# Behind the attention: order and queues of the loads, the projection out in the same block, and the borders beside the projection up

## What is computed

```
x = x + dwconv(x, pos_w, pos_b)
xn = layer_norm(x, ln1_g, ln1_b)
...                                   # q, k, v of 12 heads of 8 channels; lepe = dwconv(v, lepe_w, lepe_b)
attn = jax.nn.softmax(qk, axis=-1)
o = jnp.einsum('bnlm,bnmd->bnld', attn, vr)
o = o.transpose(0, 2, 1, 3).reshape(B, H, W, C) + lepe
x = x + (o @ out_w + out_b)
xn = layer_norm(x, ln2_g, ln2_b)
h = jax.nn.gelu(xn @ fc1_w + fc1_b, approximate=False)
h = h + dwconv(h, dw_w, dw_b)
x = x + (h @ fc2_w + fc2_b)
```

## Time and profile before

| | |
|---|---|
| median of the runs, us | 3207.21 |
| profiled execution, us | 3203.94 |
| its span, us | 3202.2 |
| mean granted clock of TensorE, share of 2.4 GHz | 0.717 |
| busy: PE, DVE, ACT, POOL | 93%, 80%, 55%, 33% |
| block behind the attention and projection out | 878.1 to 939.3 us |
| layer norm | 939.6 to 969.5 us |
| block of the borders and the gates' loads | 970.6 to 979.2 us |
| projection up starts | 979.7 us |

### The profile page before, as it was taken

The page is one execution under the profiler, slowest core; times in us unless marked ns, Lnnn a source line. Parts: engine busy times, 40 slices in busy tenths (PEclk is TensorE's granted clock), DMA queues, the critical chain, the costliest instruction groups (busy, mean ns, idle before and its releaser), DMA issues. The chain is left out here.

```text
span 3202.2 us, 127142 instructions
## 1 busy us (share of the span) xinstructions
PE 2988.6 (93%) x50420; PEld 2307.2 (72%) x50420; DVE 2551.8 (80%) x12130; ACT 1746.9 (55%) x5568; POOL 1050.1 (33%) x2510
## 2 busy tenths in 40 slices
PE   6799999999857989999999999999999999779987
PEld 3365656666523359999999999999999999455654
DVE  6799999999865678888888888888888888598872
ACT  2599999999803144444444444444444444344443
POOL 2478777778600012222222222222222222100000
PEclk8899999999968975555555555555555555689999
DMA  2323323333230000000000000000000000000000
GB/s 64 97 93 117 116 92 118 99 110 117 62 86 20 12 1 4 4 4 4 4 4 4 4 4 4 4 4 4 4 4 4 4 4 4 2 1 1 1 6 15
DMA packets 48217, 104.74 MB, mean 33 GB/s; under 512 B 11305, under 2 KB 18793, under 8 KB 47692
## 3 DMA queue, kind: packets, MB, share of 16 engines
q1 hardware_dynamic: 32796, 45.53, 5.0%
q0 software_dynamic: 13824, 50.34, 4.4%
q10 hardware_dynamic: 1072, 1.60, 0.2%
HBM read 84.06 MB, written 13.37 MB: 30 GB/s over the span
## 5 line engine op out<-in xcount | busy, mean ns | idle before, releaser
L596 PE MATMUL g_zr<-g_hp,g_wp 97*128 97x4 f16 x24576 | 1071.3, 171 | 3.3 <-DVE g_hp L648 3.2
L596 PEld LDWEIGHTS g_zr<-g_hp,g_wp 97*128 97x128 f16 x24576 | 946.0, 108 | 89.9 <-DVE g_hp L648 4.9
L686 ACT ACTIVATE g_e<-g_n 96x8 f32<-96x8 f32 x2048 | 356.5, 174 | 562.6 <-DVE g_n L635 562.6
L648 DVE TENSOR_TENSOR_SCAN g_hp<-g_gates,g_e 96x16 f16<-96x16 f32 x2048 | 384.2, 188 | 258.9 <-ACT g_e L686 180.2
L574 PE MATMUL g_zr<-s_inner,g_wi 96*128 96x64 bf16 (+1 forms) x6144 | 571.2, 234 | 3.1 <-DVE g_hs L623 3.1
L683 ACT ACTIVATE g_gates<-g_zr 96x16 f32<-96x16 f32 x2048 | 399.0, 195 | 245.0 <-PE g_zr L596 245.0
L603 PE MATMUL g_n<-g_hp,g_wp 97*128 97x8 f16 x8192 | 520.2, 174 | 0.0
L956 DVE CUSTOM_DVE_ANT_0 a_negated<-a_scores,a_mask 128x1024 f32<-128x1024 f32 x384 | 468.1, 1219 | 60.7 <-PE a_scores L874 60.1
L982 ACT ACTIVATE a_probs<-a_negated,a_negmax 128x1024 f32<-128x1024 f32 x384 | 442.3, 1152 | 18.2 <-DVE a_negmax L956 8.4
L904 PEld LDWEIGHTS a_turned<-a_ident,a_probs 128*128 128x128 f32 x3072 | 357.7, 141 | 93.8 <-ACT a_probs L982 3.6
L635 DVE TENSOR_TENSOR_SCAN g_n<-g_gates,g_n 96x24 f32<-96x24 f32 x2048 | 421.3, 206 | 2.3 <-ACT g_gates L683 2.3
(11 more groups left out here) (316 smaller groups left out, 3501.8 us busy)
## 6 DMA issues: line engine op xcount, KB each, us to landing
a_mask<-in_L_mask POOLq DMA_DIRECT2D x96, 512.0 KB, 5.3
a_k<-k_rows SPq DMA_DIRECT2D x96, 144.0 KB
a_q<-q_rows SPq DMA_DIRECT2D x96, 72.0 KB
o_parts<-a_o_sb SPq DMA_DIRECT2D x384, 18.0 KB
o_part<-o_parts SPq DMA_DIRECT2D x32, 192.0 KB
q_rows<-r_parts SPq DMA_DIRECT2D x12, 192.0 KB
k_rows<-r_parts SPq DMA_DIRECT2D x4, 576.0 KB, 3.6
out_x<-x SPq DMA_DIRECT2D x4, 384.0 KB
```

The lines of the kernel that those rows point to most:

```text
L596: mm = pe.matmul(zr_bank[u, k][:, 1 - g, d, :, at], wp[0:97, part, (2 * u + d) * NG + g, :], hp[u][0:97, d * NB:(d + 1) * NB, e], start=False,
L648: ve.tensor_tensor_scan(flat(hp[u][0:C]), keep, flat(e1[u][:, :, :]), 0.0, ALU.mult, ALU.subtract).then_inc(h1_ok[u], 1)
L686: act.activation(e1[u][:, :, 0], tn[u, k][:, :, 2], ACT.Tanh, scale=to_tanh).then_inc(n_and_zh[u], 1)
```

## The change

Behind the attention, SyncE and ScalarE each load one half: first the four denominator loads of that half, then sixteen loads of parts, image by image. There is a buffer `part` for each image, and no wait between loads. The denominators lie on 96 partitions (half, image, head), so `norm` has half the elements on each, and `head` becomes 96 x 8 x 96. GpSimd adds part 3 to part 2 of each image, VectorE part 1 to part 0, and VectorE adds the two sums and multiplies. The add to `lepe` is gone: TensorE multiplies `lepe` by `out_w` into a PSUM tensor `product` and later adds the product of `total` and `out_w` to it. VectorE takes `product` into `x` in the same block; the separate block of the projection out is gone. In `feed_forward` the block `clear` is gone: borders (all twelve strips on GpSimd) and the gates' loads stand in the block of the projection up.

```diff
-def clear(nc, tag, tensors, loads=(), loaded=None):
...
+            def borders_and_loads(block):
+                @block.sync
+                def _(sp):
+                    for dst, src in loads:
+                        sp.dma_start(dst, src).then_inc(gates["loaded"], 16)
+
+                @block.gpsimd
+                def _(po):
+                    for p in pad:
+                        for strip in border(p, 1):
+                            po.memset(strip, 0.0)
...
-            part = [sb(f"part{i}", [C, 4, 2, BANK]) for i in range(3)]
+            part = [sb(f"part{b}", [C, 4, 2, BANK]) for b in range(NB)]
...
-            norm = sb("norm", [NB * NH, 4, 2, BANK])
-            head = sb("head", [NB * NH, NB, C])
+            norm = sb("norm", [2 * NB * NH, 4, BANK])
+            head = sb("head", [2 * NB * NH, 2 * NB, C])
...
+            def loads_of(eng, half):
+                for b in range(NB):
+                    rows = (half * NB + b) * NH
+                    eng.dma_start(norm[rows:rows + NH, :, :], o_parts[:, half, b, :, 8, :]).then_inc(norm_in, 16)
+                for b in range(NB):
+                    for j in range(4):
+                        eng.dma_start(part[b][:, j, half, :], o_parts[:, half, b, j, 0:8, :]).then_inc(loaded[b], 16)
...
+                for b in range(NB):
+                    po.wait_ge(loaded[b], 16 * 8)
+                    po.tensor_tensor(part[b][:, 2], part[b][:, 2], part[b][:, 3], ALU.add).then_inc(later_ok, 1)
...
+                def beside_heads(b):
+                    if b >= 2:
+                        pe.wait_ge(taken, b - 1)
+                    for half in range(2):
+                        pe.matmul(product[b % 2][:, half, :], out_w[:, :],
+                                  lepe[:, b * L + half * BANK:b * L + (half + 1) * BANK], start=True, stop=False)
...
+                def of_heads(b):
+                    pe.wait_ge(normed, b + 1)
+                    for half in range(2):
+                        mm = pe.matmul(product[b % 2][:, half, :], out_w[:, :], total[b % 2][:, half, :], start=False,
+                                       stop=True)
+                    mm.then_inc(ready, 1)
+
+                beside_heads(0)
+                beside_heads(1)
+                pe.wait_ge(head_ok, 3)
+                pe.wait_ge(inv_ok, 1)
+                spread(0)
+                spread(1)
+                of_heads(0)
+                spread(2)
+                of_heads(1)
+                beside_heads(2)
+                spread(3)
+                of_heads(2)
+                beside_heads(3)
+                of_heads(3)
...
+                def sum_of(b):
+                    p, o = part[b], total[b % 2][:, :, :]
+                    ve.wait_ge(loaded[b], 16 * 8)
+                    ve.tensor_tensor(p[:, 0], p[:, 0], p[:, 1], ALU.add).then_inc(halved, 1)
+                    ve.wait_ge(halved, b + 1)
+                    ve.wait_ge(later_ok, b + 1)
+                    ve.tensor_tensor(o, p[:, 0], p[:, 2], ALU.add).then_inc(summed, 1)
+                    ve.wait_ge(summed, b + 1)
+                    ve.wait_ge(spread_ok, b + 1)
+                    ve.tensor_tensor(o, o, inverse[b % 2][:, :, :], ALU.mult).then_inc(normed, 1)
+
+                def take(b):
+                    ve.wait_ge(ready, b + 1)
+                    ve.scalar_tensor_tensor(x[:, cols(b)], product[b % 2][:, :, :].rearrange("c f t -> c (f t)"),
+                                            v["L0_out_b"][:, :], x[:, cols(b)], ALU.add, ALU.add).then_inc(taken, 1)
...
+                sum_of(0)
+                sum_of(1)
+                take(0)
+                sum_of(2)
+                take(1)
+                sum_of(3)
+                take(2)
+                take(3)
```

More of the change, by code:

```diff
@@ L238, in _, with project @@
             shift(3)
-def project(nc, tag, sources, weight, tiles, rows, finish, engine):
+def project(nc, tag, sources, weight, tiles, rows, finish, engine, beside=None):
     ring = 4
@@ L251, in project @@
         work = [(b, m) for b in range(NB) for m in range(tiles)]
+        if beside:
+            beside(block)
         @block.tensor
@@ L1336, in retention_block @@
-            loaded = [sem(f"loaded{i}") for i in range(3)]
-            norm_in, head_ok, halved, summed, pairs_ok, inv_ok, spread_ok, normed, added = map(
-                sem, ("norm_in", "head_ok", "halved", "summed", "pairs", "inv", "spread", "normed", "added"))
-            block = ctx.enter_context(nc.Block())
+            norm = sb("norm", [2 * NB * NH, 4, BANK])
+            head = sb("head", [2 * NB * NH, 2 * NB, C])
+            inverse = [ctx.enter_context(nc.psum_tensor(f"o_inverse{i}", [C, 2, BANK], F)) for i in range(2)]
@@ new lines, in retention_block @@
+            product = [ctx.enter_context(nc.psum_tensor(f"o_product{i}", [C, 2, BANK], F)) for i in range(2)]
+            loaded = [sem(f"loaded{b}") for b in range(NB)]
+            norm_in, head_ok, later_ok, halved, summed, pairs_ok, inv_ok, spread_ok, normed, ready, taken = map(
+                sem, ("norm_in", "head_ok", "later", "halved", "summed", "pairs", "inv", "spread", "normed", "ready",
+                      "taken"))
+            block = ctx.enter_context(nc.Block())
+            def loads_of(eng, half):
[5 more added lines that the diff above has]
+                        eng.dma_start(part[b][:, j, half, :], o_parts[:, half, b, j, 0:8, :]).then_inc(loaded[b], 16)
@@ L1341, in _ @@
             @block.sync
             def _(sp):
[L1343 to L1349, removed]
+                loads_of(sp, 0)
             @block.scalar
             def _(act):
-                for b in range(NB):
-                    for half in range(2):
-                        act.dma_start(norm[b * NH:(b + 1) * NH, :, half, :], o_parts[:, half, b, :, 8, :]
-                                      ).then_inc(norm_in, 16)
+                loads_of(act, 1)
```

47 lines of the change are left out of this document (6 added, 41 removed).

## The result

| | before | after |
|---|---|---|
| median, us | 3208.88 (four runs, 3202.97 to 3211.24) | **3182.86** (four runs, 3180.33 to 3185.76) |
| ratio, 95% interval | 1 | **0.9923** (0.9907 to 0.9938) |
| profiled execution; its span, us | 3203.94; 3202.2 | 3182.78; 3181.1 |
| attention's end to the norm's start, us | 61.5 | 42.9 |
| norm's end block to projection up, us | 9.1 | 0 |

26.0 us faster where 31.4 were forecast; the time is inside the range, 6.9 above the forecast of 3176 (1.7 of these because the median before is now 3208.88 and the forecast went from 3207.21).

A forecast was written before the change was run, and what follows sets the result against it. Bound: behind the attention a chain of denominator waits, VectorE sums and the projection out; before the projection up, SyncE's DMA issuing. Savings 22.3 + 9.1 = 31.4 us off the 3207.2 median gave 3176; range 3168 to 3190.

The forecast's parts named there:

- The second place: Between norm and projection up: the block of border memsets and gates' load issuing goes, 9.1 us saved, bounds 8.5 and 9.5.
- the loading of the parts: Block behind the attention: 6.29 MB at 298 GB/s take 21.1 us, 5.3 per image, the last complete at 906.5.
- The denominators: Start of that block: loaded alone in 5.4 us (bounds 2.7 and 11.7) plus half a microsecond to land, there at 885.4.
- no packets of parts would come before the first add: Sign in the changed kernel's trace: VectorE's first denominator add near 885.4, with no parts' packets ahead of it.
- the second rival: Denominator loads no faster, perhaps from writing only 12 partitions: 11.7 us, all behind shifts 6.3, 3182; 0.18 with two other rivals.
- The tail: Block's end: last image loaded 906.5, sums and product, last product 914.3, taken at 915.6, block ends at 917.
- slow passes: TensorE, block's end: a few passes at the slow clock among the last eight pairs move the end from 915.6 to 917.
- What is late next: In the changed block: the last image's load would be late, closely followed by VectorE, 5.0 us an image against 5.3 loading.
- The first, that the clock stays at 1.2 GHz: TensorE slow throughout the block behind the attention: 13.1 + 9.1 saved, 3185; chance 0.18 together with two other rivals.
- The third: Part loads: two queues made the mix slow, so parts go at 138 GB/s, 45.6 us, 3200; chance 0.08.
- the fourth: Part loads: two queues slow each other worse than in the mix; 120 GB/s cancels the gain, 100 gives 3218; chance 0.03.
- the fifth: Projection up's start waits for another reason than SyncE, so 9.1 us are missing: 3185; 0.18 with two other rivals.

The follow-up runs named there:

- e3: Kernel before with only the borders and gates' loads moved beside the projection up; ratio 0.9972 to the kernel before.
- e4: Kernel before with only the block behind the attention and the projection out changed; ratio 0.9942 to the kernel before.
- the first run: The changed kernel, whole change, in its first comparison with the kernel before; 3182.86 us, ratio 0.9923.
- e12: The changed kernel unaltered, profiled a third time, on the chip of the half-loads run; ratio 0.9914 to the kernel before.
- e2: The changed kernel unaltered, profiled a second time; ratio 0.9909 to the kernel before.
- e6: Changed kernel with each denominator load written to every eighth partition instead of 12 neighbouring ones; ratio 0.9906 to the kernel before.
- e1: The kernel before unaltered, profiled a second time; ratio 1.000 to itself.
- e11: Changed kernel with half the part loads left out, parts 0 and 2 each added to itself; ratio 0.9902 to the kernel before.
- e5: Changed kernel with all 32 part loads on SyncE's queue, ScalarE loading only its denominators; ratio 0.9918 to the kernel before.
- e9: Changed kernel with values and denominators stored apart in HBM, contiguous part loads, two denominator loads instead of eight; ratio 0.9924 to the kernel before.
- e10: Same as e9, but VectorE alone sums each image; ratio 0.9925 to the kernel before.
- e7: Changed kernel with GpSimd's adds removed and VectorE alone summing each image; ratio 0.9917 to the kernel before.

## Why the prediction was right, and by how much it missed

**The direction and the mechanism held**, place by place. The second place was as predicted: 9.1 forecast, 9.1 in the profiles, 9.8 in the medians of e3, whose ratio allows 5.5 to 12.5. That the stages add up to the gain (e3 and e4) held too, within the intervals.

**The term that was mis-sized is the loading of the parts.** I put it at 298 GB/s from one stretch of one execution, with no bound but one of another kind (138). The same two kernels and the variants that load in the same way gave 223 to 298 GB/s over five to ten us, at shares of 0.77 to 0.81. In the first run the parts took 25.1 us from the first add of the denominators to the last load (33.4 - 8.3) where the sum had 21.1; in e12, with the rate as read, 21.9. That is 4.0 us of the first run's difference of 5.0 at the last load.

**The denominators** were due at +7.3 and came at +8.3, +8.7 and +9.0 in the three profiles of the changed kernel. They stayed as slow as in the mix of the earlier trace rows, 134 GB/s in the view above, and they were not by themselves: by +8.0 the first run had moved 1.01 MB (0.27 in the first 2.5 us, 0.74 behind), 0.22 more than the denominators have. So the first parts went among them, against the sign that no packets of parts would come before the first add. My step counted the denominators' engine time alone, and half a microsecond for landing that no row shows: in the kernel before ScalarE's queue has its last packets between 891.5 and 892.0, and the add starts at 892.91, 0.9 us or more later. The step was 1.0 to 1.7 us short. Its upper bound, 11.7 us, is short as well: from 879.5 to 892.9, less the half microsecond, are 12.9. It only bears on the second rival.

**The tail** went the other way: 9.55 us from the last load to the norm in e2, e4, e12 and the first run alike, against 10.8 in the sum (39.2 - 28.4). From the load to the last product it took 6.0 us, as walked (915.03 to 921.02): GpSimd's add, the rest of VectorE's first add, which GpSimd had blocked, and two of 1.22. What was not needed are the 1.4 us that the sum had put on for slow passes, since TensorE was at full clock by then. So an allowance that was too large hid 1.2 us of what the loading lacked; that the total came so near is luck by this much. With these three the first run's gain is 22.3 - 1.0 - 4.0 + 1.2 = 18.5, and the profiles show 18.6 (61.5 and 42.9); for e12 it is 22.3 - 1.7 - 0.8 + 1.2 = 21.0, and they show 21.0 (61.5 and 40.5). The three pieces fill the block, so the sum has to close; what it tells is how large each miss was.

**The rest of the gap is the span around it.** The two first profiles differ by 21.1 us in span, not by 27.7 (18.6 and 9.1), since the last stage took 424.7 us in the kernel before and 431.2 in the changed one, with the same instructions, and the attention ended 3.5 us later. The other way went the norm, 1.7 us, and 1.8 us between the projection up and the last stage. In the other profiles the last stage took between 425.0 (e6) and 431.2, and 431.2 in the kernel before itself (e1). The medians of 4 to 17 runs hang less on one execution: -26.0, -30.8 and -29.4, 28.7 on average against the 31.4.

**What is late next** I had as the last load, closely followed by VectorE. Both halves were borne out, the second by e11's 0.9 us.

**The rivals.** The first, that the clock stays at 1.2 GHz, fell: in the changed kernel the granted clock was 0.52 from 895.42 to 899.40, then 1.00 to 902.5, 0.51 to 909.0 and 1.00 from 909.7 to the end of the projection. The prediction had the rise at 897.5 and no dip behind it. The dip cost little, since VectorE and the loads were later anyway. The second rival probably had the right cause, 158 ns against 95 ns a packet, but the denominators were in after 8.3 to 9.0 us and not after 13.6: the miss is 1.0 to 1.7 us, not 6.3. The third and the fourth, two queues that slow each other, fell with 295 GB/s on both; the fifth fell with the 0.04 us at 953.89.

**What stays open** is what sets the rate. It isn't the number of queues (e5), in e9 and e10 not the number of engines, the number of bytes (e11 and e12 on one chip, 296 and 295), nor the sums on GpSimd (e7 had a low rate without them). It is not simply the chip either: e6 and e7 ran on one chip, with 283 and 245. It was near constant inside some executions and rose in others, in e2 from 252 to 288, in e12 from 272 to 295, in e3 from 202 to 226. Where the scratch tensor lay in HBM and what else used that memory no row shows, and it was not tried on purpose.

## To carry to other kernels

A rate that is read from a stretch where another engine is the bound is a rate that nobody has needed yet: before a sum makes the transfers the bound, take it from several executions, and put the spread in the range. When two engines are within a microsecond of each other, taking the load off one (here half the bytes) is worth that microsecond and no more. A block that only issues DMAs and sets borders is worth its whole length when it moves beside one that does real work and lasts longer.

## What was not expected of the hardware

- At about the same share of the DMA engines, 0.77 to 0.81, the same loads went at 223, 227, 245, 254, 278, 283, 295 and 298 GB/s in different executions; with a share of 1.05 at 254 and of 1.07 at 261.
- The block between GpSimd and VectorE works in both directions. Where VectorE's add started 0.05 us before GpSimd's, the latter took 3.38 us instead of 2.35 (896.46 and 896.51 above). Where GpSimd was first, VectorE's took 2.41 instead of 1.22. The Trainium skill says so ("SBUF — State Buffer", SBUF: two separate sides): whoever starts first has the shared ports for the whole instruction. The 1.03 us more is less than the 1.22 of VectorE's add, of which 1.17 lay ahead.
- The spreading matmuls had 96 rows instead of 48, and the granted clock went from 0.50 to 1.00 while they ran, 4.0 us behind their start in the first run (895.42 to 899.40) and 5.0 to 6.8 us in the other ten profiles with 96 rows. Those of 48 rows ran 10.5 us at 0.50. Whether the rows are the reason isn't shown: TensorE had stood idle for 8.4 us before the former, behind 5.3 us of work on the position term, and for 29.5 before the latter.
- Issuing the same four denominator loads took SyncE 1.57 us in the first run and 2.40 in e5, in kernels whose lists differ only behind them.
